# Plain sums of the attention output in X, gate and x put in once per batch, and the first block of S as one fp32 matmul

## The chip, the core and the metric

The kernel runs on one core of a Trainium2 chip. A core has a matrix engine (TensorE, PE in the tables, with its weight loads as PEld), VectorE (DVE), ScalarE (ACT), GpSimd (POOL) and SyncE (SP), which here only issues DMAs. Each engine works through its own list of instructions in order and waits on semaphores. The metric is the device time of one execution in microseconds.

## The reference, cut to what matters

One layer: adaptive layer norm, causal attention with 16 heads of 128, a gated residual, layer norm again, a mixture of eight experts, a gated residual. x is 4 batches of 512 positions by 256.

```python
h = _layernorm(x) * (1 + ca) + sa
q, k, v = (einsum('ihd,bpd->biph', W, h) for W in (W_Q, W_K, W_V))    # 16 heads i, d_head 128
scores = einsum('biph,biqh->biqp', k, q)                             # 512 x 512 per batch and head
masked = scores * mask - 1e10 * (1 - mask)                           # mask: lower triangle
attn = softmax(masked / sqrt(128)); z = einsum('biqp,biph->biqh', attn, v)
x = x + ga * einsum('df,bqf->bqd', W_O, z_flat)                      # ga: one row of 256 per batch
...                                                                  # layer norm, experts, x + gb * ffn(h)
```

All is float32. The change touches the sum over heads behind W_O, `x + ga * ...`, and the first 128 x 128 block of `scores`.

## The kernel before, in words

The attention is cut into 64 units, one per head and batch; unit u has group g = u // 16 of four heads, batch b = (u % 16) // 4 and head h = u % 4 of the group. A list of events, `plan`, written by `attention_plan` and `ffn_plan`, gives the order; every engine walks the same list and issues its own part of each event. In iteration i of the loop over units the list reads: S of unit i+2, q of i+3, ri of i+2, k of i+3, norm of i+2, wo of pair i//2 - 1, ty of i+2, v, pt of i+1, z of i, tr of i+2. `fill`, `pre` and `post` place further events: layer norms (st, nm, h), weights (wh), loads (ld).

Float32 products are made of two fp32r parts: each operand is split into a high part (rounded, by ScalarE) and a low part (the rest, by VectorE, `L1140`), and `mm3` issues three passes: high x high, high x low, low x high (`L743`, `L744`, `L745`).

Events named below:

- q, k: projection of one head, 128 x 512, into one PSUM bank; ScalarE writes the high part to qk (`L698`), VectorE the low part (`L1140`), which counts up the semaphore me. qk holds one unit.
- S: scores of one unit in four query blocks i of 128 rows; block i needs keys 0 to 128(i+1). The order is blocks 0 and 2 (bank 1), 3 (bank 0), 1 (bank 2). So block 0, 128 x 128, is the first thing TensorE does in S, then block 2 with 384 columns. VectorE adds the mask and takes the extreme (`L1151`), ScalarE takes the exponential (`L634`), `norm` divides (`L683`), `ty` transposes 32 x 32 blocks (`L1167` to `L1170`), `tr` puts the blocks in place by DMA, and `pt` splits the result (`L711` on ScalarE, `L591` on GpSimd).
- z: the product with v. One of its blocks is a plain fp32 matmul of 128 columns (`L844`).
- wo: half a batch (c2) of W_O times z for pair p of units. VectorE multiplies it by the gate, from PSUM into fb (`L1187`), GpSimd adds fb to X (`L584`). X holds x at first.
- mg: the gates. GpSimd works on 4 x 512 elements in four steps (`L538` to `L544`) and writes the gate rows to memory with two DMAs (`L547`); mh reads them back for all partitions (`L551`).
- nm: the layer norm's normalisation of one batch into tmp, by VectorE (`L1116`) in batches 2 and 3.

GpSimd follows the list like the others, so what it does for an event stands behind all that it does for the events before. In the start of the list the order is: q 1, k 1, norm 0, ..., mg, tr 0, S 1, q 2, ri 1, k 2, norm 1, ty 1, pt 0, mh.

Of the kernel before, what the change touches and what calls it, by code (L numbers as in the profile page):

```python
# [20 lines left out]
FIRST_ACC = 6  # L21
EULER = 2.718281828459045
# [19 lines left out]
def unit(u):  # L42

    return u // 16, (u % 16) // 4, u % 4


def attention_plan():
# [27 lines left out]
    put(post, 60, ("wh", 20))  # L75
    plan = [("mod0",)] + [("st", 0, k) for k in range(4)] + [
# [132 lines left out]
def build(nc, x, ct, wmod, wat, wfa, wfb, cst, bcol, b2, ub, cb, out, scr, scw):  # L209
# [20 lines left out]
    with ExitStack() as ctx:  # L230
# [84 lines left out]
        s_ob, s_d0 = sem("s_ob"), sem("s_d0")  # L315
        s_pa, s_oc = sem("s_pa"), sem("s_oc")
# [84 lines left out]

        def Gs(n):
            k = (n + 2) % 5
            if k == 4:
                return G4h[:], G4l[:]
            return Gr[:, k * 1024:k * 1024 + 512], Gr[:, k * 1024 + 512:k * 1024 + 1024]
# [13 lines left out]
        def xn_at(ev):  # L420

            return stage[:, 0:1024] if ev[:2] in (("h2", 2), ("h2", 3)) else tmp[:]

# [29 lines left out]
        def _(sp):  # L453
# [16 lines left out]
            for ev in plan:  # L470
# [12 lines left out]
                elif ev[0] == "wl":  # L483
# [9 lines left out]
                    sp.dma_start(wb_at(i), scw[row:row + 1, :].broadcast_to([128, 512])).then_inc(s_wb[i % 4], 16)  # L493
                elif ev[0] == "tr":
# [21 lines left out]
        def _(pool):  # L516
# [9 lines left out]
            for ev in plan:  # L526
# [51 lines left out]
                if ev[0] == "wx" or ev[0] == "wo" and ("wx",) + ev[1:] not in plan:  # L578
# [3 lines left out]
                    if p:  # L582
                        pool.wait_ge(s_y, 2 * p + c2 - 1)
                    pool.tensor_tensor(X[:, a:a + 512], X[:, a:a + 512], fb[:, c2 * 512:c2 * 512 + 512],  # L584
                                       ALU.add).then_inc(s_y, 1)
                if ev[0] == "pt":
# [154 lines left out]
        def _(pe):  # L741
# [13 lines left out]
            for ev in plan:  # L755
# [63 lines left out]
                elif kind == "S":  # L819
                    u = ev[1]  # L820
                    pe.wait_ge(me, use[("k", u)] + 1)
                    if u == 0:
                        pe.wait_ge(s_mc, 1)
                    q = (qk[:, 0:512], qk[:, 512:1024])
                    kk = (qk[:, 1024:1536], qk[:, 1536:2048])
                    for n, (bk, chunks) in enumerate(S_ORDER):
                        if u > 0:
                            pe.wait_ge(s_E, 3 * u - 3 + n + 1)
                        for i in chunks:
                            a, w = S_AT[i][1], 128 * (i + 1)  # L830
                            ins = mm3(PS[bk][:, a:a + w], lane(q, 128 * i, 128), lane(kk, 0, w), True, True)
# [128 lines left out]
        def _(v):  # L960
# [86 lines left out]
            for ev in plan:  # L1047
# [28 lines left out]
                elif kind == "st":  # L1076
# [3 lines left out]
                    if k == 0:  # L1080
                        if n < B:
                            v.wait_ge(s_x[b], 16)
                        else:
                            v.wait_ge(s_y, 2 * (25 + 2 * b) + 2)
# [22 lines left out]
                elif kind == "nm" and ev[1:] not in ACT_NM:  # L1107
# [4 lines left out]
                    if n:  # L1112
                        v.wait_ge(mf, tmp_read[n - 1])
                    v.wait_ge(s_r0, n + 1)
# [61 lines left out]
                elif kind == "wo":  # L1176
# [3 lines left out]
                    if p:  # L1180
                        v.wait_ge(s_y, 2 * p + c2 - 1)
                    if p == 0:
                        v.wait_ge(s_g, 16)
                    if p == NU // 2 - 1:
# [41 lines left out]
                elif kind == "wt":  # L1226
                    v.wait_ge(mf, use[ev] + 1)
                    if ev[1] == 0:
                        v.wait_ge(s_y, 2 * (NU // 2 - 2) + 1)
# [163 lines left out]
```

## Time and profile before

| | |
|---|---|
| median of 3 runs | 808.82 us (807.68 to 809.59) |
| profiled execution | 808.62 us, span of its records 806.6 us |
| mean granted TensorE clock | 0.992 of full speed |
| TensorE busy | 782.7 us (97%), 4742 matmuls |
| VectorE busy | 669.6 us (83%) |
| ScalarE busy | 622.7 us (77%) |
| GpSimd busy | 423.8 us (53%) |

Busy time is an average over stages with different limits, and matmuls are pipelined, so their records overlap: a pass of 512 columns has a record of some 0.39 us, while the chain of waits counts 0.23 us until the next one takes over. For what a matmul costs, the chain or the distance between starts is to be read. The attention fills some 650 us of the span, the experts the rest.

### The profile page before, as it was taken

Reading aid. Unit: us, or ns where it says so; the run is one execution under the profiler, and the core shown is the slowest. Engines: PE = TensorE matmul, PEld = TensorE weight load, DVE = VectorE, ACT = ScalarE, POOL = GpSimd, SP = SyncE. Lnnn points to the kernel's source line nnn. Section 1 sums busy time; section 2 is a strip of 40 time slices with the busy share of each in tenths; the row PEclk is TensorE's granted clock in tenths of the full one; section 3 lists DMA queues with packets and bytes.
Section 4 is the critical chain, followed back from the end, with each engine's and each line's share of the span. In section 5 each row is a group of like instructions: output and inputs, shape, how many; then the busy total and the mean of one; then the engine's idle time right before and its main releaser. Section 6 shows DMA issues by size and latency. Waiting matters only on the chain.

```text
span 806.6 us, 14365 instructions
## 1 busy us (share of the span) xinstructions
PE 782.7 (97%) x4742; PEld 696.9 (86%) x4742; DVE 669.6 (83%) x1649; ACT 622.7 (77%) x1449; POOL 423.8 (53%) x305
## 2 busy tenths in 40 slices
PE   8899899999999999999999999999999889989997
PEld 7699898999999999999999999999999767768786
DVE  4779898888888888888888888889898988886967
ACT  3787878878787788887788887788778868865974
POOL 2455355654445555444465544465445464577654
PEclk8999999999999999999999999999999999999999
DMA  7252233343222444322344332334332131112231
GB/s 247 81 171 66 66 92 93 92 102 88 67 67 66 101 109 103 89 66 66 77 100 106 92 92 66 72 98 127 91 74 66 47 112 57 56 40 67 71 100 53
DMA packets 47592, 70.53 MB, mean 87 GB/s; under 512 B 5536, under 2 KB 38464, under 8 KB 47392
## 3 DMA queue, kind: packets, MB, share of 16 engines
q1 hardware_dynamic: 47008, 68.81, 32.4%
q8 instruction: 38, 0.62, 0.3%
q0 software_dynamic: 368, 0.81, 0.3%
q14 instruction: 34, 0.28, 0.1%
q10 hardware_dynamic: 144, 0.00, 0.0%
HBM read 25.49 MB, written 2.17 MB: 34 GB/s over the span
## 4 chain that ended last, share of the span: by engine, by line
PE 65%; ACT 16%; DVE 11%; issue 5%; POOL 2%; DMA 1%; SPq 0%; DVEq 0%; POOLq 0%
PE M L744 9%; PE M L743 9%; PE M L745 9%; PE T L743 7%; PE T L745 7%; PE T L744 7%; PE S L743 5%; PE S L745 5%; PE S L744 5%; ACT PB L634 4%; ACT PB L683 3%; DVE S L1151 2%; ACT pth L711 2%; ACT qk L698 2%; PE M L844 1%
## 5 line engine op out<-in xcount | busy, mean ns | idle before, releaser
L634 ACT ACTIVATE PB<-S,nb 128x128 f32<-128x128 f32 (+3 forms) x256 | 133.7, 532 | 110.3 <-DVE nb L1151 110.2
L584 POOL TENSOR_TENSOR X<-X,fb 128x512 f32<-128x512 f32 x64 | 83.2, 1300 | 237.3 <-DVE fb L1187 237.3
L591 POOL TENSOR_TENSOR ptl<-ptl,pth 128x896 fp32r<-128x896 f32 x126 | 179.3, 1446 | 45.9 <-ACT pth L711 45.9
L683 ACT ACTIVATE PB<-PB,ri 128x256 f32<-128x256 f32 (+3 forms) x256 | 124.5, 581 | 5.0 <-DVE ri L1160 4.9
L1151 DVE CUSTOM_DVE_ANT_0 S<-S,cc 128x128 f32<-128x128 f32 (+3 forms) x256 | 117.7, 525 | 1.3 <-PE S L745 1.3
L1140 DVE TENSOR_TENSOR qk<-M,qk 128x512 fp32r<-128x512 f32 x108 | 74.6, 691 | 45.1 <-ACT qk L698 45.1
L1167 DVE STREAM_TRANSPOSE gab<-PB 128x256 f32<-128x256 f32 (+2 forms) x192 | 109.4, 622 | 0.5 <-DMA ptl<-gab 0.4
L743 PE MATMUL S<-qk 128*128 128x128 f32 (+3 forms) x256 | 84.0, 328 | 4.5 <-DVE qk L1140 4.5
L743 PE MATMUL M<-hh,W 128*128 128x512 f32 x222 | 87.1, 392 | 0.8 <-DVE hl L1126 0.8
L745 PE MATMUL M<-hh,W 128*128 128x512 f32 x222 | 87.7, 395 | 0.0
L744 PE MATMUL M<-hl,W 128*128 128x512 f32 x222 | 87.6, 395 | 0.0
L744 PE MATMUL S<-qk 128*128 128x128 f32 (+3 forms) x256 | 83.0, 324 | 0.0
L745 PE MATMUL S<-qk 128*128 128x128 f32 (+3 forms) x256 | 82.8, 323 | 0.0
L711 ACT CAST pth<-ptl 128x896 fp32r<-128x896 f32 (+1 forms) x128 | 81.4, 699 | 0.9 <-DMA ptl<-gab 0.9
L698 ACT CAST qk<-M 128x512 fp32r<-128x512 f32 x108 | 64.1, 593 | 3.8 <-PE M L745 2.7
L743 PE MATMUL M<-pth,vh 128*128 128x512 f32 x177 | 65.1, 368 | 1.9 <-DVE rt L991 1.1
L744 PE MATMUL M<-ptl,vh 128*128 128x512 f32 x177 | 60.2, 340 | 0.0
L745 PE MATMUL M<-pth,vl 128*128 128x512 f32 x177 | 59.9, 339 | 0.0
L745 PE MATMUL T<-W,zt 128*128 128x256 f32 x204 | 57.3, 281 | 0.0
L743 PE MATMUL T<-W,zt 128*128 128x256 f32 x204 | 57.1, 280 | 0.0
L744 PE MATMUL T<-W,zt 128*128 128x256 f32 x204 | 57.1, 280 | 0.0
L743 PEld LDWEIGHTS S<-qk 128*128 128x128 f32 x256 | 48.6, 190 | 9.4 <-DVE qk L1140 5.6
(261 smaller groups left out, 2430.3 us busy)
## 6 DMA issues: line engine op xcount, KB each, us to landing
ptl<-gab SPq DMA_DIRECT2D x256, 160.0 KB, 3.1
stage<-in_wat SPq DMA_DIRECT2D x16, 512.0 KB, 5.2
gab<-scw SPq DMA_DIRECT2D x16, 256.0 KB, 3.2
tmp<-scw SPq DMA_DIRECT2D x16, 256.0 KB, 3.5
X<-in_x SPq DMA_DIRECT2D x3, 512.0 KB, 8.0
stage<-in_wfa SPq DMA_DIRECT2D x3, 512.0 KB, 4.8
out<-X SPq DMA_DIRECT2D x3, 512.0 KB, 2.7
X<-in_wmod SPq DMA_DIRECT2D x1, 1024.0 KB, 13.1
```

The lines of the kernel that those rows point to most:

```text
L584: pool.tensor_tensor(X[:, a:a + 512], X[:, a:a + 512], fb[:, c2 * 512:c2 * 512 + 512], ALU.add).then_inc(s_y, 1)
L591: pool.tensor_tensor(pt_part(lo, c), pt_part(lo, c).bitcast(F32), pt_part(hi, c).bitcast(F32), ALU.subtract).then_inc(s_pl, 1)
L634: ins = act.activation(PB[:, P_OFF[i]:P_OFF[i] + w], PS[bk][:, a:a + w], ACT.Exp, bias=nb[:, i:i + 1], scale=-1.0, accum_out=sm[:, i:i + 1])
L683: act.activation(p, p, ACT.Copy, scale=ri[:, i:i + 1]).then_inc(s_P3, 1)
L698: act.copy(dst, src).then_inc(mh, 1)
L711: act.copy(pt_part(pth[u % 2], c), pt_part(ptl[u % 2], c).bitcast(F32)).then_inc(s_ph, 1)
L743: pe.matmul(o, lhs[0], rhs[0], start=start, stop=False, **kw)
L744: pe.matmul(o, lhs[0], rhs[1], start=False, stop=False, **kw)
L745: return pe.matmul(o, lhs[1], rhs[0], start=False, stop=stop, **kw)
L1140: v.tensor_tensor(lo, src, hi.bitcast(F32), ALU.subtract).then_inc(me, 1)
L1151: ins = v.tensor_tensor_reduce(PS[bk][:, a:a + w], PS[bk][:, a:a + w], mask[:, 512 - w:512], -INV, BIG, ALU.add, ALU.min, nb[:, i:i + 1])
L1167: v.transpose(Y_blocks(i, i + 1), P_blocks(i, 0, i + 1))
```

## The change

Two things change.

First, the sum over heads. For the pairs p below 24 (`GATED`), VectorE no longer multiplies by the gate: it adds W_O's product out of PSUM to X (for the very first pair of a batch it copies it), so X holds a plain sum, and GpSimd's addition of fb goes. New events `cv` multiply the sum by the gate and add x, on GpSimd, in two halves per batch; x is loaded again by new events `xr` (SyncE's queue) into tmp or fb. Pairs from 24 on work as before.

Second, for units 1 to 48 (`ONE_PIECE`), block 0 of S is one fp32 matmul of unsplit q and k. GpSimd makes these: high part plus low part, 128 x 128, once in event q and once in event k, into rt (unused until the router). TensorE waits for both (semaphore s_q0) before the first matmul of S.

```diff
@@ -19,6 +19,8 @@
+ONE_PIECE = range(1, 49)
+GATED = 24
...
+    for b in range(B):
+        put(post, (36, 37, 42, 45)[b], ("xr", b))
+        put(post, (38, 42, 46, 48)[b], ("cv", b, 0))
+        put(post, (40, 44, 47, 49)[b], ("cv", b, 1))
...
+        first_block = {"q": rt[:, 0:128], "k": rt[:, 128:256]}
...
+        def x_again(b):
+
+            return (tmp, fb)[b % 2]
...
+                elif ev[0] == "xr":
+                    b = ev[1]
+                    if b == 0:
+                        sp.wait_ge(mf, use[("h", B - 1, 1)] + 1)
+                    elif b == 1:
+                        sp.wait_ge(s_gd, 32)
+                    else:
+                        sp.wait_ge(s_cv, 4 * (b - 1))
+                    sp.dma_start(x_again(b)[:], x[:, b * 1024:b * 1024 + 1024]).then_inc(s_xr, 16)
...
-                if ev[0] == "wx" or ev[0] == "wo" and ("wx",) + ev[1:] not in plan:
+                if ev[0] == "cv":
+
+                    _, b, c2 = ev
+                    y = X[:, b * 1024 + c2 * 512:b * 1024 + c2 * 512 + 512]
+                    y2 = y.rearrange("p (a n) -> p a n", a=2)
+                    ga = gab[:, b * 256:b * 256 + 256].rearrange("p (a n) -> p a n", a=1)
+                    if b == 0:
+                        pool.wait_ge(s_g, 16)
+                    pool.wait_ge(me, use[("wo", GATED - 8 + 2 * b + 1, c2)] + 1)
+                    pool.tensor_tensor(y2, y2, ga.broadcast_to([128, 2, 256]), ALU.mult).then_inc(s_cv, 1)
+                    pool.wait_ge(s_xr, 16 * b + 16)
+                    pool.wait_ge(s_cv, 4 * b + 2 * c2 + 1)
+                    pool.tensor_tensor(y, y, x_again(b)[:, c2 * 512:c2 * 512 + 512], ALU.add).then_inc(s_cv, 1)
+                if ev[0] == "wx" or ev[0] == "wo" and ev[1] >= GATED and ("wx",) + ev[1:] not in plan:
                     _, p, c2 = ev
                     a = unit(2 * p)[1] * 1024 + c2 * 512
                     pool.wait_ge(me, use[("wo", p, c2)] + 1)
-                    if p:
-                        pool.wait_ge(s_y, 2 * p + c2 - 1)
+                    if p % 2 == 0:
+                        pool.wait_ge(s_cv, 4 * unit(2 * p)[1] + 2 * c2 + 2)
+                    else:
+                        pool.wait_ge(s_y, added(p - 1, c2))
                     pool.tensor_tensor(X[:, a:a + 512], X[:, a:a + 512], fb[:, c2 * 512:c2 * 512 + 512],
                                        ALU.add).then_inc(s_y, 1)
+                if ev[0] in ("q", "k") and ev[1] in ONE_PIECE:
+                    o = (ev[0] == "k") * 1024
+                    pool.wait_ge(me, use[ev] + 1)
+                    pool.tensor_tensor(first_block[ev[0]], qk[:, o:o + 128].bitcast(F32), qk[:, o + 512:o + 640].bitcast(F32),
+                                       ALU.add).then_inc(s_q0, 1)
...
+                    if u in ONE_PIECE:
+                        pe.wait_ge(s_q0, 2 * ONE_PIECE.index(u) + 2)
...
@@ -828,7 +878,10 @@
                             pe.wait_ge(s_E, 3 * u - 3 + n + 1)
                         for i in chunks:
                             a, w = S_AT[i][1], 128 * (i + 1)
-                            ins = mm3(PS[bk][:, a:a + w], lane(q, 128 * i, 128), lane(kk, 0, w), True, True)
+                            if i == 0 and u in ONE_PIECE:
+                                pe.matmul(PS[bk][:, a:a + w], first_block["q"], first_block["k"], start=True, stop=True)
+                            else:
+                                ins = mm3(PS[bk][:, a:a + w], lane(q, 128 * i, 128), lane(kk, 0, w), True, True)
                         ins.then_inc(s_S, 1)
...
+                    if n == B:
+                        v.wait_ge(s_cv, 4 * B)
...
                     v.wait_ge(mf, use[ev] + 1)
-                    if p:
-                        v.wait_ge(s_y, 2 * p + c2 - 1)
-                    if p == 0:
+                    if p < GATED:
+                        y = X[:, b * 1024 + c2 * 512:b * 1024 + c2 * 512 + 512]
+                        if p < 8 and p % 2 == 0:
+                            v.tensor_copy(y, bank(ev)[:]).then_inc(me, 1)
+                        else:
+                            v.wait_ge(me, use[("wo", p - 1 if p % 2 else p - 7, c2)] + 1)
+                            v.tensor_tensor(y, y, bank(ev)[:], ALU.add).then_inc(me, 1)
+                        continue
+                    if p == GATED:
                         v.wait_ge(s_g, 16)
+                        v.wait_ge(s_cv, 14 + 2 * c2)
+                    else:
+                        v.wait_ge(s_y, added(p - 1, c2))
                     if p == NU // 2 - 1:
                         v.wait_ge(s_ws[0], 16)
                     ga = gab[:, b * 256:b * 256 + 256].rearrange("p (a n) -> p a n", a=1)
```

In the changed file line numbers are shifted: L632 is GpSimd's addition for block 0, L882 the plain matmul, L615 and L618 the two steps of cv, L639 what was L591, L604 what was L576, L791 to L793 what were L743 to L745.

GpSimd at the start of the list, from unit 0's weights on. Before (rt is the new operands' tile, ptl and pth the split P, scr the gates' place in memory):

```order
L531 TENSOR_TENSOR rs<-rs 128x4
L538 TENSOR_SCALAR gab<-fb 4x512
L540 TENSOR_TENSOR gab<-fb,gab 4x512
L542 TENSOR_SCALAR gab<-gab 4x512
L544 TENSOR_TENSOR fb<-gab 4x512
L547 DMA scr<-fb 4x256 x2
L591 TENSOR_TENSOR ptl0<-ptl0,pth0 128x4x224
```

The same place after:

```order
L559 TENSOR_TENSOR rs<-rs 128x4
L632 TENSOR_TENSOR rt<-qk 128x128 x2
L566 TENSOR_SCALAR gab<-fb 4x512
L568 TENSOR_TENSOR gab<-fb,gab 4x512
L570 TENSOR_SCALAR gab<-gab 4x512
L572 TENSOR_TENSOR fb<-gab 4x512
L575 DMA scr<-fb 4x256 x2
L632 TENSOR_TENSOR rt<-qk 128x128 x2
L639 TENSOR_TENSOR ptl0<-ptl0,pth0 128x4x224
```

The first pair of additions is unit 1's, ahead of the gates; the second is unit 2's, behind the gates' four operations and two DMA issues.

GpSimd in units about 40, two iterations with a weight piece (W). Before:

```order
L591 TENSOR_TENSOR ptl0<-ptl0,pth0 128x4x224
L591 TENSOR_TENSOR ptl0<-ptl0,pth0 128x4x64
L576 TENSOR_TENSOR W1<-stage,W1 128x1024
L584 TENSOR_TENSOR X<-X,fb 128x512
L591 TENSOR_TENSOR ptl1<-ptl1,pth1 128x4x224
```

After:

```order
L639 TENSOR_TENSOR ptl0<-ptl0,pth0 128x4x64
L604 TENSOR_TENSOR W1<-stage,W1 128x1024
L632 TENSOR_TENSOR rt<-qk 128x128 x2
L639 TENSOR_TENSOR ptl1<-ptl1,pth1 128x4x224
L639 TENSOR_TENSOR ptl1<-ptl1,pth1 128x4x64
L615 TENSOR_TENSOR X<-X,gab 128x512
L618 TENSOR_TENSOR X<-X,tmp 128x512
L632 TENSOR_TENSOR rt<-qk 128x128 x2
```

The additions for q and k stand where the addition to X stood, ahead of pt; a cv pair stands behind pt and ahead of the next unit's additions.

TensorE at the head of S in unit 1, before (S1 is bank 1, M0 the bank that v is written to):

```order
L745 MATMUL M0<-W0,hl 128x256
L743 MATMUL S1<-qk 128x128
L744 MATMUL S1<-qk 128x128
L745 MATMUL S1<-qk 128x128
L743 MATMUL S1<-qk 128x384
```

The same place after (rt holds the unsplit q and k):

```order
L793 MATMUL M0<-W0,hl 128x256
L882 MATMUL S1<-rt 128x128
L791 MATMUL S1<-qk 128x384
L792 MATMUL S1<-qk 128x384
L793 MATMUL S1<-qk 128x384
```

Three passes of block 0 have become one instruction; the rest of S follows as before.

## Rows read from the trace of the kernel before

**Rows 1.** Stretches: length, busy us (count) by engine, clock, DMA share, GB/s

```profile
12.00:16.00 4.00, 3.85 (x31) 3.62 (x28) 1.27 (x2) 2.00 (x3) 1.66 (x1) 0.57 0.95 379
39.40:42.80 3.40, 3.40 (x12) 2.74 (x11) 3.30 (x11) 3.08 (x8) 3.08 (x4) 0.51 0.19 28
200.00:300.00 100.00, 100.00 (x638) 91.90 (x637) 83.62 (x204) 79.77 (x202) 51.81 (x36) 1.00 0.33 82
```

**Rows 2.** Timeline (start, us, engine), TensorE, S's first pass: units 2, 11, 15, 17, 31, 48

```profile
38.29 0.33 PE L743 MATMUL S<-qk 128*128 128x128 f32 x1 [1.99 <-DVE qk L1140]
...
129.45 0.33 PE L743 MATMUL S<-qk 128*128 128x128 f32 x1 [1.09 <-DVE qk L1140]
...
166.93 0.22 PE L743 MATMUL S<-qk 128*128 128x128 f32 x1
...
185.61 0.22 PE L743 MATMUL S<-qk 128*128 128x128 f32 x1
...
316.37 0.22 PE L743 MATMUL S<-qk 128*128 128x128 f32 x1
...
475.15 0.22 PE L743 MATMUL S<-qk 128*128 128x128 f32 x1
```

**Rows 3.** Chain of waits, 70 to 120 us, shares by engine and line

```profile
by line: ACT PB L683 18.6%; ACT PB L634 12.9%; issue 12.0%; DVE S L1151 9.7%; ACT pth L711 9.2%; DVE tmp L1116 6.8%; ACT qk L698 5.7%; ACT vh L698 3.5%; ACT zt L698 3.5%; ACT hh L676 3.4%; ACT T L677 2.9%; DVE qk L1140 2.3%; DVE nb L1151 2.
```

**Rows 4.** Chain of waits in order of time (start, us, what), units 2 to 3

```profile
38.29 0.33 PE S L743
...
50.17 0.49 PE M L793 x4
```

**Rows 5.** Timeline, VectorE, k's low part of units 11, 15 and 31

```profile
128.70 0.69 DVE L1140 TENSOR_TENSOR qk<-M,qk 128x512 fp32r<-128x512 f32 x1 [0.30 <-ACT qk L698]
...
166.05 0.69 DVE L1140 TENSOR_TENSOR qk<-M,qk 128x512 fp32r<-128x512 f32 x1 [0.30 <-ACT qk L698]
...
313.37 0.69 DVE L1140 TENSOR_TENSOR qk<-M,qk 128x512 fp32r<-128x512 f32 x1 [0.30 <-ACT qk L698]
```

**Rows 6.** Chain of waits, unit 30, z's plain block and S's first passes

```profile
306.61 0.22 PE M L844 x2
...
307.19 0.06 PE S L743
...
307.48 0.23 PE S L743
307.70 0.18 PE S L744
```

**Rows 7.** Groups by form (count, busy us, mean ns), TensorE's weight loads

```profile
L743 PEld LDWEIGHTS S<-qk 128*128 128x128 f32 x256 | 48.6, 190 | 9.4 <-DVE qk L1140 5.6 <-issue 0.9
...
L844 PEld LDWEIGHTS M<-ptl,v 128*128 128x128 f32 x118 | 21.4, 188 | 0.0
```

**Rows 8.** Groups by form, GpSimd's additions and subtractions

```profile
L584 POOL TENSOR_TENSOR X<-X,fb 128x512 f32<-128x512 f32 x64 | 83.2, 1300 | 237.3 <-DVE fb L1187 237.3
L591 POOL TENSOR_TENSOR ptl<-ptl,pth 128x256 fp32r<-128x256 f32 x63 | 47.9, 761 | 0.0
```

**Rows 9.** Timeline, GpSimd, the gates: first operation and DMA issues

```profile
33.77 1.96 POOL L538 TENSOR_SCALAR gab<-fb 4x512 f32<-4x512 f32 x1 [7.18 <-DVE fb L1062]
...
40.73 1.18 POOL L547 DMA_DIRECT2D scr<-fb  x2 [0.29 <-POOL fb L544]
```

**Rows 10.** Groups by form, VectorE, the gate's multiplication

```profile
L1187 DVE TENSOR_TENSOR fb<-T,gab 128x512 f32<-128x512 f32 x51 | 34.7, 681 | 0.0
```

**Rows 11.** Line 1116: duration ns min/median/max, first and last start

```profile
L1116 DVE TENSOR_SCALAR tmp<-X,mv,rs x18: 398/541/1882, 7.1 to 605.7; 128x256 f32<-128x256 f32 x18
```

**Rows 12.** Timeline, VectorE, batch 3's normalisation

```profile
105.33 2.21 DVE L1116 TENSOR_SCALAR tmp<-X,mv,rs 128x256 f32<-128x256 f32 x2
```

**Rows 13.** Timeline, GpSimd, a weight piece, and P's low part after unit 30's S

```profile
104.62 2.44 POOL L576 TENSOR_TENSOR W<-stage,W 128x1024 fp32r<-128x1024 f32 x1
...
307.03 2.83 POOL L591 TENSOR_TENSOR ptl<-ptl,pth 128x896 fp32r<-128x896 f32 x2 [0.56 <-ACT pth L711]
```

More of the change, by code:

```diff
@@ L44, in unit, with added @@
     return u // 16, (u % 16) // 4, u % 4
+def added(p, c2):
+    return 2 * (p - GATED) + c2 + 1
 def attention_plan():
@@ L315, in build @@
         s_ob, s_d0 = sem("s_ob"), sem("s_d0")
+        s_q0 = sem("s_q0")
+        s_xr, s_cv = sem("s_xr"), sem("s_cv")
         s_pa, s_oc = sem("s_pa"), sem("s_oc")
@@ L1083, in _ @@
                         else:
-                            v.wait_ge(s_y, 2 * (25 + 2 * b) + 2)
+                            v.wait_ge(s_y, added(GATED + 1 + 2 * b, 1))
                         if n:
@@ L1228, in _ @@
                     if ev[1] == 0:
-                        v.wait_ge(s_y, 2 * (NU // 2 - 2) + 1)
+                        v.wait_ge(s_y, added(NU // 2 - 2, 0))
                     else:
```

## Prediction

> **What bounds the kernel now.** I read the table of stretches first. From 200 to 300 us TensorE is busy for 100.00 of 100.00 us [rows 1], and I went on to its matmuls. The first matmul of S starts at 185.61 in unit 17 and at 316.37 in unit 31 [rows 2]: 130.76 us over 14 units, 9.34 us each, and (475.15 - 316.37)/17 = 9.34 up to unit 48. There TensorE is the bound, and time taken off it shortens the kernel.
>
> Before unit 12 it is not so. The chain of waits from 70 to 120 us consists of ScalarE, VectorE and issue time [rows 3]: mask, exponentials, casts of q and k, normalisation and transposes of one head, handed back and forth, are the bound, and TensorE waits at the places where it needs their result. One such wait is unit 11's S, 1.09 us on the low part of k [rows 2]. Before that lies a start-up stretch, 38 to 66 us, in which the chain runs through TensorE again, from unit 2's S to the transposes before unit 3's [rows 4]. Then I asked, for each unit, how long before S its k was ready: VectorE's subtraction ends at 129.39, 166.74 and 314.06 in units 11, 15 and 31 [rows 5], TensorE starts at 129.45, 166.93 and 316.37 [rows 2]. The margins are 0.06, 0.19 and 2.31 us. A new wait of half a microsecond is felt in units 10 to 16 and hidden later.
>
> **Part 1, the first block as one matmul.** Now it is three passes of 128 columns: from 307.19 to 307.48 in the chain, 0.29 us, and the 384-column pass behind them holds it 0.23 where its sisters hold it 0.18 [rows 6], because weights for the short passes load one behind the other. So the block costs 0.29 + 0.05 = 0.34. One matmul of unsplit fp32 with 128 columns stands in z: two records, 0.22 us in the chain [rows 6]. Saving 0.34 - 0.22 = 0.12; I take 0.11, half of two to three passes of 0.11. Bounds: 0.06 if the pass behind stays at 0.23, and 0.17 if also the load ahead of it is hidden.
>
> The trace shows a weight load of 188 ns for the fp32 operand and 190 ns for the split one [rows 7], so nothing of the gain is lost there. The Trainium skill (TensorE: Matmul & The Clock Gate, "Weight-path perf modes — Fast Weight Load (FWL) and DoubleRow") says that the fast weight load is off when the input type is FP32. By that rule the plain block could be the slower one; the two rows do not show such a difference, and the case is rival D.
>
> **Part 2, GpSimd's two additions per unit.** 128 x 128 each. The nearest rows: 256 columns take 761 ns and 512 take 1300 [rows 8], 2.1 ns a column, so 761 - 269 = 0.49 us. In a unit both take 1.0 us and the 1.30 us addition to X goes, so GpSimd has less to do. But S now waits for k's addition: 0.49 plus some 0.08 to begin and be seen, 0.57 us after the moment at which it could start before. In units 17 to 48 the margin covers it. In unit 15 (margin 0.19) it does not. Worked through with 9.23 us a unit from TensorE and the unchanged k times: S is late by 0.57 in unit 11, gains 0.22 in the next two, is held again by k in units 13 and 15, and unit 17 starts 0.57 - 0.22 = 0.35 us later than it would. From there 31 units and unit 48's own block give 32 x 0.11 = 3.5. Part 1 and 2 from unit 11 on: -3.5 + 0.35 = -3.2 us. Units 1 to 10 give nothing, since TensorE waits there anyway.
>
> **Part 3, unit 2.** GpSimd works in order. The additions for unit 2 are behind the four gate operations and two DMA issues. In the trace of before the gate work starts at 33.77, and its two issues last from 40.73 to 41.91 [rows 9]. Unit 2's k is ready when S starts at 38.29, so now the two additions run from 41.91, 0.95 us, and S starts at about 42.9 instead of 38.29: +4.6. Behind the waiting S on TensorE are q, k and v of the next units and batch 1's transposes at 50.17, for which VectorE waits before it masks unit 3. That is the chain [rows 4], so the delay goes through, less the 0.11 of unit 2's own block: +4.5. Nothing after it waits for the clock of another resource: the loads are long ahead. This is the term that sets the sign. Bounds: 4.2 to 4.8.
>
> The granted clock is 0.51 from 39.4 to 42.8 [rows 1], half speed at 1.2 GHz, after TensorE had stood idle for 1.99 us before 38.29 [rows 2]. Half speed for 3.4 us costs 1.7. With an idle time of 6.6 us there will be such a stretch again; I take the same 1.7, net zero, and keep from -1.7 (it falls into the idle time) to +1.7 (it lasts twice as long).
>
> **Part 4, VectorE and its neighbour.** wo's multiplication out of PSUM (681 ns [rows 10]) becomes an addition out of PSUM of the same shape, or, 8 times, a copy; both read one PSUM and at most one SBUF operand: nothing, at worst 0.02 a unit beside TensorE. The normalisation of x, a VectorE operation of 398 ns at best, takes up to 1882 ns [rows 11]. Two of them last 2.21 us from 105.33, while GpSimd's weight subtraction holds from 104.62 to 107.06 [rows 12, 13]. q's addition now comes directly behind such work, inside the normalisation of batches 2 and 3, in the stretch that VectorE and ScalarE bound. That is two places with up to 0.49 each: I take 0.4, bounds 0 and 1.0. The Trainium skill (SBUF — State Buffer, "Who interferes with whom") says that tensor_scalar in a two-port mode and a GpSimd instruction exclude each other for the whole of an instruction. The trace agrees in that the 2.21 us end just behind the subtraction. By that rule the loss is at most one addition at each place.
>
> **Part 5, x again and the gates.** Eight multiplications and eight additions of 512 columns, 1.30 each, fall into units in which GpSimd has over 3 us to spare; 48 additions of 1.30 go (16 remain). They come in front of the next unit's additions: GpSimd's work on P starts with S at 307.03 and takes 2.83 [rows 13], and with such a pair it ends 5.4 us after S, while k is ready at 314.06 [rows 5], 7.0 us after it. Four loads of 512 KB, as the weight loads, stand behind the transposes' DMAs and are read a unit or more later. Cost nothing; without this cover 0.5 a unit for eight units.
>
> **Sum.** Profiled execution: 808.62 us, of which 806.6 is span and 2.0 lies around it. -3.2 + 4.5 + 0.4 = +1.7: 810.3. The median of the runs is 0.2 higher, 808.82, so 810.5.
>
> **Rivals.**
> A. The start-up delay is made up, because VectorE and ScalarE have slack between units 2 and 5, or the gate work ends sooner. For it: before 38 us these two also wait. Against it: the chain from 38.29 to 50.17 runs in TensorE's matmuls without a wait. It gives 808.8 - 3.2 + 0.4 = 806.0.
> B. The half-speed stretch costs 1.7 more after 6.6 us of idle time. For it: between 12 and 16 us, after the first idle times, the clock is granted at 0.57 still [rows 1], so a half-speed stretch need not end when work resumes. It gives 812.2.
> B'. It falls into the idle time: 810.5 - 1.7 = 808.8.
> C. The additions lengthen the VectorE-ScalarE loop of units 1 to 16 (two normalisations blocked for 1.0 in all, and S's delay of 0.57 reaching the loop twice). Against it: from S to its mask there are some 4 us. It gives 808.8 + 4.5 + 2.1 - 3.2 + 0.6 = 812.8.
> D. The plain matmul saves only 0.06. 32 x 0.06 = 1.9, less a hold of 0.45: -1.5. It gives 808.8 + 4.5 + 0.4 - 1.5 = 812.2. The weight-load rows speak against it.
>
> **Chances.** My forecast (809.2 to 812.0 as its own range) 0.48, A 0.12, B 0.14, B' 0.10, C 0.07, D 0.09. No change means within 0.2% or 1.6 us, about what can be told from nothing here: 807.2 to 810.4. The forecast lies just at its upper edge; some two fifths of its chance fall below. Slower: 0.29 + 0.14 + 0.07 + 0.09, less a little = 0.53. Same: 0.19 + 0.10 + some of A = 0.34. Faster 0.13. The range of 806.0 to 813.2 leaves out part of A and of C and D.
>
> **What would show it.** Unit 2's S starting near 42.9 behind two GpSimd additions of 0.49, where before it was 38.29; a period of 9.23 us in units 17 to 48 and 9.34 after; one idle time of TensorE per unit in 11, 13 and 15; the fp32 matmul at 0.22 in the chain. The prediction is wrong if unit 3's S is not about 4.5 us late, if the period stays at 9.34, or if TensorE waits for the additions in most units.

## The result and the profile after

| | before | after |
|---|---|---|
| median (range), runs | 807.94 us (805.07 to 809.82), 20 | 810.87 us (808.15 to 812.78), 20 |
| profiled execution: span, mean granted clock | 806.6 us, 0.992 | 809.2 us, 0.988 |
| TensorE busy, matmuls | 782.7 us, 4742 | 778.0 us, 4694 |
| VectorE / ScalarE / GpSimd busy | 669.6 / 622.7 / 423.8 us | 670.6 / 620.8 / 425.7 us |

The ratio is 1.0034 with an interval of 1.0024 to 1.0045: 2.75 us slower (1.9 to 3.6), where 1.7 was forecast. TensorE is busy for 4.7 us less, and yet the kernel takes longer.

The stretches of after, as [rows 1] (length, busy us and count by engine, granted clock, DMA share, GB/s):

```profile
8.00:12.00 4.00, 3.43 (x38) 3.44 (x38) 1.50 (x5) 2.07 (x3) 0.13 (x1) 0.95 1.03 401
12.00:16.00 4.00, 3.78 (x21) 2.87 (x21) 2.32 (x4) 2.76 (x4) 1.41 (x1) 0.62 0.99 401
39.10:45.90 6.80, 4.96 (x15) 4.41 (x16) 2.40 (x9) 1.89 (x5) 6.75 (x8) 0.51 0.54 143
97.20:100.60 3.40, 3.40 (x14) 2.97 (x13) 3.04 (x10) 3.40 (x11) 0.49 (x2) 0.54 0.23 72
200.00:300.00 100.00, 100.00 (x633) 91.49 (x632) 83.81 (x208) 79.91 (x206) 47.94 (x46) 1.00 0.35 84
```

Half speed (1.2 GHz) lasts 6.8 us at 39.1, twice as long as in before, and there is a new stretch of 3.4 us at 97.2. Between 8 and 12 us this execution is granted 0.95, the one of before 0.58. Over the 20 runs of the changed kernel the median of the granted clock is 0.988; the profiled execution of before has 0.992, and so have its runs beside the experiments below, in the median. In what follows a half-speed stretch is one in which the granted clock is about 0.5.

Timeline of GpSimd and then of TensorE around unit 2, answering [rows 2, 9] (start, us, engine, line, operation, idle time before it and its releaser):

```profile
31.80 1.96 POOL L566 TENSOR_SCALAR gab<-fb 4x512 f32<-4x512 f32 x1 [5.08 <-DVE fb L1115]
37.20 1.27 POOL L572 TENSOR_TENSOR fb<-gab 4x512 f32<-4x512 f32 x1
38.77 1.18 POOL L575 DMA_DIRECT2D scr<-fb  x2 [0.29 <-POOL fb L572]
39.97 0.87 POOL L632 TENSOR_TENSOR rt<-qk 128x128 f32<-128x128 f32 x2
...
40.94 0.76 PE L882 MATMUL S<-rt 128*128 128x128 f32 x2 [6.69 <-issue]
41.35 0.67 PE L791 MATMUL S<-qk 128*128 128x384 f32 x1
```

Gates, DMA issues, the two additions, S: each starts within 0.3 us of the end of the one before it. TensorE stands idle for 6.69 us. The profile calls the releaser "issue", though 40.94 lies just behind the end of the second addition (39.97 + 0.87 = 40.84).

Where GpSimd has nothing in the way, the wait is small. Timelines of VectorE, GpSimd and TensorE at unit 7, and TensorE at units 17 and 48:

```profile
89.79 0.69 DVE L1195 TENSOR_TENSOR qk<-T,qk 128x512 fp32r<-128x512 f32 x1 [0.30 <-ACT qk L746]
90.56 0.46 POOL L632 TENSOR_TENSOR rt<-qk 128x128 f32<-128x128 f32 x1 [1.15 <-DVE qk L1195]
91.12 0.46 PE L882 MATMUL S<-rt 128*128 128x128 f32 x2 [0.79 <-DVE X L1241]
...
191.41 0.38 PE L882 MATMUL S<-rt 128*128 128x128 f32 x2
191.54 0.42 PE L791 MATMUL S<-qk 128*128 128x384 f32 x1
...
477.16 0.42 PE L791 MATMUL S<-qk 128*128 128x384 f32 x1
```

In unit 7 the low part of k ends at 90.48 and S starts 0.64 us later, 0.58 more than the 0.06 of unit 11 in before. The releaser in brackets (an addition into X on VectorE) is again only an operation that ran at the time. Between units 3 and 48 TensorE stands idle ahead of S in units 7, 9, 10 and 11, for 0.79, 0.31, 0.34 and 1.55 us; in before it does so in unit 11 alone, for 1.09. From unit 17 on S has no idle time ahead of it, and (477.16 - 191.54)/31 = 9.213 us a unit against 9.34: 0.126 less. After unit 48 the distance is 9.34 again.

The chain of waits in unit 30, answering [rows 6]:

```profile
311.22 0.12 PE M L793
311.34 0.22 PE S L882 x2
311.56 0.18 PE S L791
311.74 0.17 PE S L792
```

Laid over each other by the start of S's first 384-column pass in each unit, the two executions differ by the following (us, after less before; the last column is a matmul of the experts' part, at 662.00 us in before and 664.43 in after):

| unit | 0 | 1 | 2 | 3 | 4 | 6 | 7 | 8 | 11 | 17 | 48 | 63 | 664 us |
|---|---|---|---|---|---|---|---|---|---|---|---|---|---|
| later by | -1.97 | -2.09 | 2.67 | 3.02 | 3.01 | 2.78 | 3.70 | 5.04 | 5.96 | 5.65 | 1.73 | 1.64 | 2.43 |

### The profile page after: what moved, and what is told of

It is laid out like the page before. It is cut to its first block, busy times and chain, and to the rows that moved or that the text cites. A ratio compares the mean times of both kernels' runs of the same rounds, so it can differ in the third digit from the quotient of the medians.

```text
span 809.2 us, 14293 instructions
## 1 busy us (share of the span) xinstructions
PE 778.0 (96%) x4694; PEld 691.0 (85%) x4694; DVE 670.6 (83%) x1649; ACT 620.8 (77%) x1449; POOL 425.7 (53%) x369
## 4 chain that ended last, share of the span: by engine, by line
PE 65%; ACT 16%; DVE 11%; issue 4%; POOL 2%; DMA 1%; SPq 0%; DVEq 0%; POOLq 0%
PE M L792 9%; PE M L793 9%; PE M L791 9%; PE T L791 7%; PE T L793 7%; PE T L792 7%; PE S L791 4%; PE S L793 4%; PE S L792 4%; ACT PB L682 3%; ACT PB L731 3%; ACT pth L759 2%; DVE S L1206 2%; ACT qk L746 2%; PE S L882 1%
## 5 line engine op out<-in xcount | busy, mean ns | idle before, releaser
L639 POOL TENSOR_TENSOR ptl<-ptl,pth 128x896 fp32r<-128x896 f32 x126 | 179.4, 1446 | 113.0 <-ACT pth L759 113.0
L632 POOL TENSOR_TENSOR rt<-qk 128x128 f32<-128x128 f32 x96 | 44.4, 463 | 124.7 <-DVE qk L1195 124.7
L793 PE MATMUL M<-hh,W 128*128 128x512 f32 x222 | 88.2, 397 | 0.0
L791 PE MATMUL M<-hh,W 128*128 128x512 f32 x222 | 87.4, 394 | 0.2 <-DVE hl L1181 0.2
L791 PE MATMUL S<-qk 128*128 128x128 f32 (+3 forms) x208 | 74.0, 356 | 1.4 <-DVE qk L1195 1.4
L792 PE MATMUL S<-qk 128*128 128x128 f32 (+3 forms) x208 | 69.8, 335 | 0.0
L793 PE MATMUL S<-qk 128*128 128x128 f32 (+3 forms) x208 | 69.7, 335 | 0.0
L791 PE MATMUL M<-pth,vh 128*128 128x512 f32 x177 | 65.1, 368 | 1.9 <-DVE rt L1044 1.1
L793 PE MATMUL M<-pth,vl 128*128 128x512 f32 x177 | 59.9, 339 | 0.0
L793 PE MATMUL T<-W,zt 128*128 128x256 f32 x204 | 57.3, 281 | 0.0
L791 PE MATMUL T<-W,zt 128*128 128x256 f32 x204 | 56.9, 279 | 0.0
L792 PE MATMUL T<-W,hh 128*128 128x256 f32 x200 | 56.6, 283 | 0.0
```

What stands on the lines that cost most here:

```text
L632: pool.tensor_tensor(first_block[ev[0]], qk[:, o:o + 128].bitcast(F32), qk[:, o + 512:o + 640].bitcast(F32), ALU.add).then_inc(s_q0, 1)
L639: pool.tensor_tensor(pt_part(lo, c), pt_part(lo, c).bitcast(F32), pt_part(hi, c).bitcast(F32), ALU.subtract).then_inc(s_pl, 1)
L791: pe.matmul(o, lhs[0], rhs[0], start=start, stop=False, **kw)
L792: pe.matmul(o, lhs[0], rhs[1], start=False, stop=False, **kw)
L793: return pe.matmul(o, lhs[1], rhs[0], start=False, stop=stop, **kw)
```

## The experiments

All are compared with the kernel before on the same chip; its median was 807.7 us beside the first four kernels, 807.9 beside the next four and 807.3 beside the last two. "The whole change" is the changed kernel, 810.9 us.

**Where the single matmul begins.** Three kernels that differ in one line from the whole change:

```
-ONE_PIECE = range(1, 49)
+ONE_PIECE = range(3, 49)      # e1_from3
+ONE_PIECE = range(0)          # e2_sums_only
+ONE_PIECE = range(17, 49)     # e4_from17
```

> The whole change, but the plain first block and its additions only in units 3 to 48. Theory Q (unit 2's S waits behind the gate work on GpSimd, 4.6 us, and what follows is smaller): unit 2's S starts some 1.99 us after TensorE ran dry, as before, instead of 6.7; the half-speed stretch at 42 us costs 1.7 instead of 2.5; in all 4.6 to 6 us less than the whole change, 805 to 806.5, so 2 to 3 us faster than before. Theory L (additions in units 3 to 16 and their ports are the larger cost): at most 2 us less than the whole change, about 809.

Measured: 805.6 us (12 runs), ratio 0.9967 (0.995 to 0.9984). Leaving out two of 48 units takes off 5.3 us and turns the sign. TensorE's wait before unit 2's S is back at the length of before:

```profile
36.43 0.43 PE L791 MATMUL S<-qk 128*128 128x128 f32 x1 [1.95 <-DVE qk L1195]
```

> Only the plain sums, gate and x put in once per batch; S as before, no additions of q and k. Theory Q: no change, 807.5 to 808.5, with units 17 to 48 at 9.34 us. Rival P (the plain sums themselves cost something: the copy and addition on VectorE, x loaded again, eight pairs of multiply and add on GpSimd): 1 us or more slower than before, to be seen in units 36 to 49 or 5 to 16.

Measured: 810.0 us (12 runs), ratio 1.0008 (0.9997 to 1.002). The median is above the 807.5 to 808.5 that I expected, and the interval includes no change. The runs lie in two groups, at about 808 and 810.1. The profiled one is of the upper group; its units take 9.34 us, and what it has more than before are a half-speed stretch in unit 8 (13.57 us for that unit instead of 11.72) and one near 693 us. This kernel has no additions of q and k at all, so a half-speed stretch in unit 8 does not need them. The sums cost little by themselves, at most 0.2%.

> The whole change, but the plain first block and its additions only in units 17 to 48, where k is ready early. Theory Q: no wait for an addition anywhere, 32 x 0.126 = 4.0 us faster than before, 803.5 to 804.5, and 1.5 to 2.5 us faster than with units 3 to 48, because the stretch of units 5 to 16 loses nothing to additions. Theory that units 3 to 16 lose nothing to the additions: equal to the kernel with units 3 to 48 within 0.5 us.

Measured: 804.0 us (6 runs), ratio 0.9946 (0.993 to 0.9963), as expected. The profiled run is the slowest of the six, 808.4, with a half-speed stretch of 3.4 us in unit 8, again without an addition near it. It is 1.6 us below the kernel that begins at unit 3, but the two intervals overlap: that units 3 to 16 cost anything is not shown by this pair.

**The wait without the gain.** The additions and waits stay, the matmul goes back to three passes:

```
-                            if i == 0 and u in ONE_PIECE:
-                                pe.matmul(PS[bk][:, a:a + w], first_block["q"], first_block["k"], ...)
-                            else:
-                                ins = mm3(...)
+                            ins = mm3(...)
```

> The whole change, with the additions and TensorE's wait for them, but block 0 of S still in three passes (the sums made by GpSimd are not used). Theory Q: what the additions and the wait cost by themselves: units 17 to 48 at 9.34 us again, so 32 x 0.126 = 4.0 us more than the whole change, 814 to 815.5. Rival M (the gain of the plain matmul is partly eaten elsewhere): less than 3 us above the whole change.

Measured: 814.4 us (6 runs), ratio 1.0085 (1.0064 to 1.0106). It is 3.6 us over the whole change; 32 units at 0.126 are 4.0. The waits are the loss and the matmul is the gain: in this kernel the distance between units is 9.34 us from unit 17 to 48. Timeline and stretch around unit 2:

```profile
41.17 0.45 PE L791 MATMUL S<-qk 128*128 128x128 f32 x1 [6.56 <-issue]
...
39.00:50.00 11.00, 8.83 (x34) 7.73 (x35) 3.59 (x13) 4.61 (x13) 8.17 (x9) 0.61 0.37 110
```

The same idle time is followed here by 10.2 us at half speed, and there is none at 97.

**The gain without the wait.** The matmul takes the high parts of q and k as they are, and the kernel leaves the low parts out of that block; the additions and S's wait for them are gone:

```
-                                pe.matmul(..., first_block["q"], first_block["k"], ...)
+                                pe.matmul(..., qk[:, 0:128].bitcast(F32), qk[:, 1024:1152].bitcast(F32), ...)
```

> The first query block of units 1 to 48 is one fp32 matmul of the high parts of q and k alone: GpSimd adds nothing up, S waits for nothing new, and the low parts are left out of that block's result. The plain sums in X stay. If the saving of TensorE (0.126 us a unit) is taken in each of the 48 units: 807.9 - 48 x 0.126 = 801.9. If units 1 to 16 go at the pace of the ScalarE and VectorE loop, as the chain of before says, only the 32 units from 17 on pay: 807.9 - 4.0 = 803.9, as for the kernel that begins at unit 17, and GpSimd's additions then cost nothing beyond unit 2. My expectation lies between, 802.5 to 804.3. If an fp32 matmul on q and k were slower than one on the sums, or stood in the way, it would be over 805.

Measured: 804.6 us (12 runs), ratio 0.9964 (0.995 to 0.9978), just above the range expected (802.5 to 804.3), at the end at which only units 17 on pay. With 32 more additions and their waits in units 1 to 16 absent, it is no faster than the kernel that begins at unit 17. VectorE's low part of k and TensorE's S in unit 11:

```profile
129.43 0.69 DVE L1189 TENSOR_TENSOR qk<-M,qk 128x512 fp32r<-128x512 f32 x1 [0.30 <-ACT qk L741]
130.18 0.49 PE L875 MATMUL S<-qk 128*128 128x128 f32 x2 [1.08 <-DVE qk L1189]
```

S starts 0.06 us behind k here (129.43 + 0.69 = 130.12), but from unit 11 to unit 17 this kernel needs 55.78 us, the whole change 55.74 and before 56.05. The 0.5 to 0.6 us that an addition puts ahead of S is a lateness of that S, not a longer unit.

**The clock by itself.** The whole change, with idle TensorE kept at work in two places ("filled" from here on). The results are overwritten:

```
+                    if u == 2:
+                        pe.wait_ge(s_E, 4)
+                        fill(PS[1][:, 0:128], 80)      # 80 bf16 matmuls of 128 columns
...
+                    if ev == ("q", 8):
+                        fill(o[:, 0:128], 24)
```

> The whole change, with idle TensorE filled in two places: 80 bf16 matmuls of 128 columns (about 6.2 us at 77 ns each) ahead of the S of unit 2, and 24 (1.85 us) ahead of the q of unit 8, where the profile of the whole change shows idle times of 6.69 and 1.98 us and the granted clock at half just after. Their results are overwritten. If the clock falls because of these idle times, there is no half-speed stretch after either: 2.5 + 1.2 = 3.7 us less, 807.2; if only the one at unit 8 goes, 809.7. If the clock falls by something else, the time stays at 810.9, or grows where the filling outlasts the wait. Expected 807 to 809.5, and windows at 1.0 at 41 to 46 and 97 to 101 us.

Measured: 807.1 us (12 runs), ratio 0.9993 (0.9976 to 1.001), 3.8 us below the whole change (3.3 by the two ratios); 3.7 was the working. The 80 matmuls take 4.64 us from 36.35, behind 2.11 us in which TensorE is still idle. S of unit 2 starts at the same time as without them, and the clock does not fall (timeline, then stretches):

```profile
39.33 1.67 PE L799 MATMUL S<-Dz 128*128 128x128 bf16 x27
40.93 0.49 PE L891 MATMUL S<-rt 128*128 128x128 f32 x2
...
39.00:46.00 7.00, 7.00 (x63) 6.29 (x61) 3.06 (x11) 3.64 (x12) 6.95 (x8) 1.00 0.53 139
97.00:101.00 4.00, 4.00 (x31) 3.86 (x30) 3.82 (x13) 4.00 (x11) 0.67 (x2) 1.00 0.00 0
```

Distances between 384-column passes in five profiled executions tell what a half-speed stretch costs here (us; "before filled" is the last experiment below):

| | before | before filled | whole change | whole change filled | three passes, wait kept |
|---|---|---|---|---|---|
| half speed near unit 2 | 3.4 | none | 6.8 | none | 10.2 |
| unit 2 to 3 | 12.10 | 10.49 | 12.45 | 10.38 | 13.18 |
| unit 1 to 4 | 28.43 | 28.14 | 33.53 | 31.35 | 34.30 |

At unit 3 the stretch of before has cost 1.6, but at unit 4 only 0.3 is left of it. Without it TensorE is early and waits for VectorE, whose operation stands behind a chain that runs from 36 to 50 us mostly through ScalarE's exponentials, divisions and casts (timeline of before filled, between units 3 and 4):

```profile
51.49 0.51 PE L743 MATMUL T<-hh,W 128*128 128x512 f32 x1 [0.85 <-DVE hl L1138]
```

Behind the long wait that slack is used up (the filled whole change has no idle time there), and the stretch counts almost in full, 2.2 at unit 4. The wait itself costs 31.35 - 28.14 = 3.2 there, not the 4.6 by which S is late.

**How far the gain reaches.** The single matmul in units 17 to 57, and in units 17 to 62 with the filling ahead of unit 8:

```
+ONE_PIECE = range(17, 58)     # e7_17_to_57
+ONE_PIECE = range(17, 63)     # e8_best, with fill(o[:, 0:128], 24) at q of unit 8
```

> One matmul in units 17 to 57 instead of 17 to 48. Nine units more, in which GpSimd also has a piece of W (2.4 us) and an addition into X (1.3) besides the low part of P (2.8). If the two additions of 0.46 us find room there: 804.0 - 9 x 0.126 = 802.9 (802.5 to 803.5), with a period of 9.21 us to unit 57. If they come behind a piece of W and S waits for them: units 49 to 57 at 9.34 or more, 804.0 to 806.

Measured: 804.8 us (801.2 to 806.5, 9 runs), ratio 0.9959 (0.9944 to 0.9974). The distance between units is 9.21 up to unit 57 in the profiled execution, as expected, but the median is above the range given (802.5 to 803.5) and not below that of units 17 to 48. The profiled run is the fastest of its nine, at 801.2. A gain of 1.1 can't be told apart in a scatter of 5 us. This execution is not filled, and yet, behind the same idle time ahead of unit 2's S, it has no half-speed stretch:

```profile
36.31 0.33 PE L791 MATMUL S<-qk 128*128 128x128 f32 x1 [1.96 <-DVE qk L1195]
...
36.00:50.00 14.00, 13.64 (x86) 12.07 (x86) 11.52 (x28) 13.66 (x30) 12.16 (x10) 1.00 0.42 105
```

> One matmul in units 17 to 62, and 24 filling matmuls ahead of the q of unit 8. Against the kernel with units 17 to 48 (804.0): 14 units more at 0.126 is 1.8, of which units 58 to 62 (9.76 us each at present, so held by something other than TensorE) may give nothing, so -1.1 to -1.8; the filling takes up to 1.2 us where there was a half-speed stretch in unit 8. Expected 801.0 to 802.9. If filling does nothing: 802.3 to 802.9.

Measured: 804.3 us (802.0 to 806.0, 7 runs), ratio 0.9952 (0.9932 to 0.9973), short of the expectation. Units 59 and 60 take 10.26 and 9.96 us instead of 9.75 and 9.73 with three passes: there 0.5 and 0.2 us are lost again, where the additions were put in. The filling of 24 did nothing visible: both this and the kernel without it had no half-speed stretch at unit 8 (12.02 and 12.06 us).

**Taking the scatter away.** Four idle places filled: 24 matmuls more at the start, 24 ahead of unit 2's S, 26 ahead of unit 8's q, 34 at about 720 us. Once with the single matmul in units 17 to 57, once in the kernel before with nothing else changed.

```
-WARM = 60, 16, 12
+WARM = 84, 16, 12
...
+                    if j == 0 and t == 2:
+                        pe.wait_ge(s_gl, n - 3)
+                        fill(HID_AT[n % 4][:, 0:128], 34)
```

> One matmul in units 17 to 57, and TensorE filled with bf16 matmuls of 128 columns whose results are overwritten, in four idle places of the profile: 24 more at the start (idle 2.26 us before 8.57), 24 ahead of the S of unit 2 (idle 1.99), 26 ahead of the q of unit 8 (2.08), 34 at about 720 us (3.05). With one matmul in units 17 to 57 alone the profiled run has a span of 799.4 us and two half-speed stretches, 3.4 us each, and the median of the runs is 804.8. If the scatter of the runs (801.2 to 806.5) comes from half-speed stretches behind those idle times, the filled kernel stays near the low end, at 799.5 to 802. If the clock's stretches do not follow the idle times, the median stays at 804 to 805.

> The kernel before, with the same filling in the same four places and nothing else changed. The profile of before has half-speed stretches at the start (6.8 us), at 39.4 (3.4) and at about 723 (3.4); each 3.4 us of them costs up to 1.7 us. If they follow the idle times: 807.9 less 2 to 5, 803 to 806, and against the filled kernel with one matmul in units 17 to 57 the difference is 41 x 0.126 = 5.2 us. If they do not: 807.9.

Measured: 802.2 us (801.7 to 803.2, 6 runs), ratio 0.9937 (0.9917 to 0.9957), the lowest median of all, with an interval that overlaps those of the unfilled kernels from unit 17 on; and 805.1 us (804.25 to 805.98, 12 runs), ratio 0.9971 (0.996 to 0.9982). The scatter falls from 4.6 us (before, on this chip) to 1.4 and 1.7. The first median is 0.2 us above the range given (799.5 to 802), the second is inside its own; their difference of 2.9 us is not the 5.2 that I put beside them. In the profiles they are 5.3 apart at unit 57 and 3.6 at the end: the faster kernel loses 0.6 in units 60 to 63 and about 1.0 by the first matmul of the experts. Stretches of before, and of before filled:

```profile
36.00:50.00 14.00, 12.01 (x70) 10.66 (x69) 11.26 (x26) 13.53 (x33) 12.39 (x10) 0.88 0.30 87
715.00:735.00 20.00, 16.95 (x77) 13.64 (x76) 16.22 (x35) 12.66 (x22) 10.41 (x9) 0.91 0.26 81
```

```profile
12.00:16.00 4.00, 3.83 (x23) 3.02 (x21) 2.37 (x3) 2.85 (x5) 1.49 (x1) 0.60 0.95 366
36.00:50.00 14.00, 13.33 (x91) 12.07 (x89) 11.53 (x26) 13.68 (x32) 12.75 (x10) 1.00 0.39 100
715.00:735.00 20.00, 19.67 (x121) 16.12 (x120) 16.97 (x38) 14.59 (x25) 11.38 (x9) 1.00 0.20 71
```

The stretches at 39 and 723 us are gone; the one at 12 to 16 us is not, in spite of the 24 more ahead of it, and both filled kernels have one of 3.4 us that the profile of before has not, at 687 and 691 us. That filling raises the clock is seen over the runs: 0.995 to 1.0 in the 12 runs of before filled, 0.988 to 0.996 in the 17 of before.

## Why the prediction was right, and where its terms were off

**Part 1, the matmul: right, a little small.** I took 0.11 a unit, it is 0.126: the chain has 0.22 + 0.18 where it had 0.29 + 0.23, the whole 0.12 of the working, and I had rounded down. Rival D (0.06) falls. By the Trainium skill (TensorE: Matmul & The Clock Gate, "Weight-path perf modes — Fast Weight Load (FWL) and DoubleRow") the fast weight load is off for FP32 weights. No cost of that shows here: the matmul takes 0.22 us in the chain, as its sister in z did before.

**Part 2, GpSimd's additions: the price right, its reach wrong.** The addition takes 463 ns (forecast 490), and S starts 0.58 us later where it stands directly behind k. I had named units 11, 13 and 15 and then charged unit 17 with 0.35 for them. That charge was not there: from unit 11 to 17 the kernel without additions takes 55.78 us and the whole change 55.74, so a late S in these units makes none of them longer. From unit 11 on the change gives 5.96 - 1.73 = 4.2 us, where I had 3.2; the 31 periods to unit 48 are 3.9 of it. But TensorE waits in units 7, 9, 10 and 11, and not in 13 and 15, and in units 7 to 10 the waits cost something, under part 4.

**Part 3, unit 2: the delay of S right, its way through wrong twice.** From unit 1 to unit 2's 384-column pass the time grows from 8.35 to 13.11, 4.8 us; forecast 4.6 before the block's own 0.11. S starts at 40.94 and not 42.9 only since this execution is 2.0 us early from its start. The order on GpSimd is as forecast, and leaving units 1 and 2 out takes 5.3 us off, the largest single effect of all. But the delay doesn't go through whole, as I had it: at full clock 3.2 of it is left at unit 4. I had read the chain of before, which runs in TensorE's matmuls from 38.29 to 50.17, as proof that there is no slack; it runs there because of the half-speed stretch, and without the stretch it runs through ScalarE. And "net zero" for the clock is wrong: the stretch became 6.8 us long and costs 2.2 at unit 4, where the one of before costs 0.3. The two errors, 1.4 and 1.9, nearly cancel: 28.43 to 33.53 from unit 1 to 4 is 5.1, and I had 4.5.

**Part 4, VectorE and ScalarE in units 4 to 16: the sign right, 0.4 forecast, 2.6 found.** The time from unit 4's 384-column pass to unit 17's parts it: 127.13 us in before, 127.18 without additions, 128.11 with the whole change and TensorE filled, 129.77 in the whole change. So the plain sums and the matmul together do nothing here (0.05), the additions cost 0.93, within my bounds of 0 and 1.0, and 1.66 is the clock. A second pair without a half-speed stretch in unit 8 gives the additions the same price: 128.29 with three passes and the wait kept, 127.33 in the kernel of units 17 to 57, 0.96. The half-speed stretch at 97.2 was not in my working: before has the same idle time ahead of it (2.08 us, 1.98 in after) and keeps its clock. It lengthens unit 8 to 13.06 us (11.48 filled). That the change brought this stretch about is not shown: the kernel with the sums alone and the one that begins at unit 17 have it too (129.16 and 129.11 from unit 4 to 17), and the one with three passes and the wait kept has none. At the place that I had named, the normalisation of batch 3, its four operations have shifted against GpSimd's work (timelines of VectorE and GpSimd, answering [rows 12, 13]):

```profile
108.26 3.43 DVE L1171 TENSOR_SCALAR tmp<-X,mv,rs 128x256 f32<-128x256 f32 x2
111.61 0.68 DVE L1195 TENSOR_TENSOR qk<-T,qk 128x512 fp32r<-128x512 f32 x1
112.21 0.87 DVE L1171 TENSOR_SCALAR tmp<-X,mv,rs 128x256 f32<-128x256 f32 x2
...
109.09 2.45 POOL L604 TENSOR_TENSOR W<-stage,W 128x1024 fp32r<-128x1024 f32 x1
```

Line 1171 is line 1116 of before. Four operations take 4.30 us instead of 3.63. The first now takes 1.02 us and ends 0.16 us behind P's low part on GpSimd; the second takes 2.49 and ends at 111.69, 0.15 us behind the weight piece; one of the last pair runs beside an added short operation and takes 0.55 instead of 0.40. By the Trainium skill (SBUF — State Buffer, "Who interferes with whom") an operation of VectorE in a two-port mode and one of GpSimd block each other until the one that came first is over, and the trace agrees. The neighbour that held the longest is the weight piece and not the added operation: what shifted is where the two meet. In the kernel that begins at unit 3, which has the added operations here too, the same four take 1.16 and 2.35 us.

**What no part held.** Two items, and they are about as large as the terms. The start: S of unit 0 is 1.97 us early in this execution, granted 0.95 instead of 0.58 from 8 to 12 us. The ten kernels without more matmuls at the start had unit 0's 384-column pass anywhere from 20.3 to 23.2 us, with nothing changed ahead of it, so I take it for chance of the run and no effect. And the end: after unit 63 the changed kernel loses another 0.8. The experts' first matmul, in before and after:

```profile
630.80 0.50 PE L743 MATMUL S<-ur,W 128*128 128x512 f32 x1 [0.83 <-DVE ur L1298]
```

```profile
632.80 0.50 PE L791 MATMUL S<-ur,W 128*128 128x512 f32 x1 [1.19 <-DVE ur L1362]
```

The idle time is 0.83 and 0.84 in the two kernels with the sums of before, and 1.18 or 1.19 in the ten others, the one with the sums alone among them. So these 0.36 us belong to the half with the plain sums. The other 0.4 is idle time at 646 us, 1.19 against 0.78 in before; it varies from 0.74 to 1.19 among the ten and is 0.84 in before filled, so it can't be put down to the change. What makes VectorE late there is open: its operations are the same, in the same order.

**The sum.** By the table: -2.1 (up to unit 1), + 5.1 (to unit 4: wait 3.2, clock 1.9), + 2.6 (to unit 17: additions 0.9, clock 1.7), - 3.9 (to unit 48), - 0.1, + 0.8 (end) = 2.4 of the 2.6 between the spans. Without the start and the clock it is + 1.0. The two filled kernels say much the same: the whole change filled is slower than before filled by 1.3 us of span, and by 1.8 by their ratios to before, though one has two filled places and the other four. So the wait does set the sign, as forecast, but only about half of the loss stands at full clock.

The rest is the clock, and the runs bear this out. The median granted clock is 0.988 in the whole change and 0.989 with three passes and the wait kept, the two unfilled kernels in which unit 2 waits; it lies from 0.992 to 0.994 in before, in the five other unfilled kernels and in the one filled at unit 8 alone. The 0.004 less, of 809 us, is an estimate of at most 3.2 us. The forecast of 1.7 came out near 2.75 since what it lacked in loss (the clock, the additions in units 7 to 10, the end) was set off by what it lacked in gain (1.0), by the slack that it didn't see (1.4) and, in the profiled execution, by the early start; the nearness of the number is in part luck.

Of the rivals, A (the start-up delay is made up) holds for 1.4 of the 4.6 us, at full clock. B (the clock costs 1.7 more) holds: 1.9 more at unit 4. My own forecast had neither. B' falls: the stretch is longer. C (the additions lengthen the loop, 2.1) holds at less than half its price, 0.93; the 0.6 that stands in its sum besides has no source in the working.

## What to carry to other kernels

An addition on an idle engine costs what stands ahead of it in that engine's queue on the worst occasion, not its mean share. Here 94 of the 96 additions of 0.46 us cost 0.9 us together. The two behind the chain of gates cost some 5, with what the clock added, which is more than the whole gain of 4. Start such a scheme where the fed engine is the bound and the feeding one is free (units 17 to 57 here), and leave the start-up as it was. A chain of waits read in a stretch at half speed shows TensorE as the bound where at full clock another engine may be. And fill the idle gaps of TensorE before fine comparisons: the same two kernels scatter by 1.4 and 1.7 us instead of 5.3 and 4.6.

## What the runs showed of the hardware

- The granted clock fell to 1.2 GHz in stretches of 3.4, 6.8 or 10.2 us, most of them after TensorE had been idle for 2 to 7 us. The same idle time was followed by a stretch in one execution and not in another: ahead of unit 2's S 1.99 us in before with one, 1.96 in the kernel of units 17 to 57 without; in unit 8 2.08 us in before without, 1.98 in after with one, 2.44 in the kernel of units 17 to 57 without; 6.69 us before unit 2 with 6.8 us of half speed, and 6.56 with 10.2.
- A stretch of 3.4 us at half speed cost 1.6 us one unit on and 0.3 us two units on where ScalarE's chain had slack to give, and one of 6.8 us cost 2.2 where a wait had used the slack up.
- One stretch had no idle time ahead of it. In the kernel of units 17 to 57 filled (and, between 686 and 694 us, in six others, not in before) the clock falls at 687 us, behind sixteen matmuls of 16 columns. Its timeline, first and last of them and the next passes of 512 columns, at 0.23 and then at 0.43 us each:

```profile
684.96 0.28 PE L933 MATMUL M<-W,hh 128*128 128x16 f32 x1
...
686.65 0.26 PE L934 MATMUL M<-W,hl 128*128 128x16 f32 x1
686.77 0.48 PE L791 MATMUL S<-ur,W 128*128 128x512 f32 x1
...
688.20 0.63 PE L792 MATMUL T<-Gr,W 128*128 128x512 f32 x1
688.63 0.63 PE L793 MATMUL T<-Gr,W 128*128 128x512 f32 x1
...
690.73 0.40 PE L792 MATMUL T<-Gr,W 128*128 128x512 f32 x1
```

- Throw-away bf16 matmuls of 128 columns in the idle time delayed nothing (S of unit 2 at 40.93 with 80 of them, 40.94 without), and behind them the clock stayed at 2.4 GHz in the profiled executions. In before, in all four places, they raise the median of the runs' granted clock from 0.992 to 0.9985, are worth 0.3% (2.1 us between the medians) and take the scatter from 4.6 to 1.7 us.
- An fp32 matmul of 128 columns, in two records, takes 0.22 us in the chain, and three split passes with their effect on the next take 0.34; putting the one in place of the three took 0.126 us off each unit.
